# Selective scan: convolution folded into the projection, batch 1 prepared inside the loop, GpSimd takes part of the C products

## The reference

```
x  = norm(x)                      # L0a: RMS norm; L3a: layer norm with weight and bias
u, z = split(x @ W_in)            # 256 channels each
u  = silu(sum_j u[t-3+j] * conv_w[:, j] + conv_b)      # causal convolution, 4 taps
dt, B, C = split(u @ W_xproj)     # rank 8 (L0a) or 1 (L3a), 16 and 16
dt = softplus(dt @ W_dt + dt_bias)
for n in 16 states:               # a recurrence over the 512 positions
    s_n[t] = s_n[t-1] * exp(dt[t] * A_n) + dt[t] * u[t] * B_n[t]
    y[t]  += s_n[t] * C_n[t]
out = ((y + u * D) * silu(z)) @ W_out
```

## Time and profile before

| | us |
|---|---|
| median of 3 runs | 3445.13 (3442.0 to 3448.75) |
| profiled execution, its own time | 3442.52 |
| its span, first to last instruction | 3440.9 |
| busy PE, DVE, ACT, POOL | 2647.8, 1726.3, 1450.1, 576.3 |
| mean granted TensorE clock | 0.893 |

### The profile page before, as it was taken

The page is one execution under the profiler, slowest core; times in us unless marked ns, Lnnn a source line. Parts: engine busy times, 40 slices in busy tenths (PEclk is TensorE's granted clock), DMA queues, the critical chain, the costliest instruction groups (busy, mean ns, idle before and its releaser), DMA issues. The chain is left out here.

```text
span 3440.9 us, 33444 instructions
## 1 busy us (share of the span) xinstructions
PE 2647.8 (77%) x11658; PEld 1159.7 (34%) x11666; DVE 1726.3 (50%) x2715; ACT 1450.1 (42%) x2368; POOL 576.3 (17%) x564
## 2 busy tenths in 40 slices
PE   3567778999879789466745677889997897985677
PEld 1221264444334233123212212735443442431232
DVE  3867541555131721695648675425552227127955
ACT  2443502655234444443425445036552344444444
POOL 0432000000002411260006220000000024113500
PEclk8898968999979899799878989599999898997998
DMA  2002000000010210000000020000000102100000
GB/s 100 0 0 63 12 1 0 1 1 1 0 49 0 75 50 0 0 0 1 1 13 0 1 66 9 1 0 1 1 1 1 49 4 72 49 0 0 0 2 7
DMA packets 36752, 54.59 MB, mean 16 GB/s; under 512 B 7648, under 2 KB 19936, under 8 KB 36576
## 3 DMA queue, kind: packets, MB, share of 16 engines
q1 hardware_dynamic: 32224, 48.42, 4.3%
q10 hardware_dynamic: 4352, 3.94, 0.4%
HBM read 38.44 MB, written 13.63 MB: 15 GB/s over the span
## 5 line engine op out<-in xcount | busy, mean ns | idle before, releaser
L1709 ACT ACTIVATE L1b_pr<-ps,L1b_mneg 128x512 f32<-128x512 f32 x256 | 173.7, 683 | 195.7 <-DVE L1b_mneg L1748 195.7
L518 POOL TENSOR_TENSOR xs<-xs,L2f_part 128x512 f32<-128x512 f32 x32 | 40.5, 1265 | 1286.7 <-DVE L2f_part L507 1286.7
L90 ACT ACT_TABLE_LOAD x34 | 43.6, 1283 | 412.1 <-PEq L671 180.5
L1746 DVE TENSOR_REDUCE L1b_m<-ps 128x2 f32<-128x1024 f32 x128 | 156.8, 1225 | 105.0 <-PE ps L1613 101.0
L1046 POOL TENSOR_TENSOR L3a_db<-L3a_du,L3a_bs 128x1024 f32<-128x1024 f32 x64 | 150.4, 2354 | 225.2 <-ACT L3a_bs L1017 214.7
L1046 POOL TENSOR_TENSOR L0a_db<-L0a_du,L0a_bs 128x1024 f32<-128x1024 f32 x64 | 150.4, 2354 | 224.0 <-ACT L0a_bs L1017 213.5
L1416 ACT ACTIVATE L0b_pt<-ps 128x1024 f32<-128x1024 f32 x128 | 129.3, 1024 | 117.6 <-PE ps L1316 115.5
L1504 DVE TENSOR_REDUCE L0b_mx<-ps 128x1 f32<-128x512 f32 x256 | 159.0, 683 | 36.7 <-PE ps L1303 35.2
L1772 DVE COPY L1b_prt<-ps 128x512 f32<-128x512 f32 x128 | 88.5, 692 | 124.9 <-PE ps L1624 124.6
L1122 DVE TENSOR_TENSOR_SCAN L0a_hs<-ps,L0a_db 128x1024 f32<-128x1024 f32 x64 | 146.1, 2282 | 9.6 <-ACT ps L1009 8.0
L1122 DVE TENSOR_TENSOR_SCAN L3a_hs<-ps,L3a_db 128x1024 f32<-128x1024 f32 x64 | 146.1, 2283 | 9.4 <-ACT ps L1009 8.0
(11 more groups left out here) (556 smaller groups left out, 5471.1 us busy)
## 6 DMA issues: line engine op xcount, KB each, us to landing
L2f_w<-expert_dram SPq DMA_DIRECT2D x32, 256.0 KB, 3.0
L2g_w<-expert_dram SPq DMA_DIRECT2D x32, 256.0 KB, 3.0
weights<-w_dram SPq DMA_DIRECT2D x7, 852.5 KB, 9.3
L0b_qs<-stack_dram SPq DMA_DIRECT2D x32, 96.0 KB, 2.2
stack_dram<-L0b_cut SPq DMA_DIRECT2D x24, 128.0 KB, 2.2
L2b_qs<-stack_dram SPq DMA_DIRECT2D x32, 96.0 KB, 2.2
stack_dram<-L2b_cut SPq DMA_DIRECT2D x24, 128.0 KB, 2.1
L0b_ks<-stack_dram SPq DMA_DIRECT2D x28, 96.0 KB, 2.3
```

The lines of the kernel that those rows point to most:

```text
L1709: act.activation(pr[:, s % 2, h, :], g.ps[:, 2 * (s % 2) + h, :], ACT.Exp, bias=mneg[:, s % 2, h:h + 1], accum_out=total[:, u % 2, t, h:h ...
L1746: dve.tensor_reduce(m[:, s % 2, :], g.ps[:, 2 * (s % 2):2 * (s % 2) + 2, :], AX.X, ALU.max).then_inc(max_raw, 1)
```

## The change

- `prepare`: the blob of weights holds, for each block, the four taps repeated over 128 partitions (`_taps`, 1024 columns in place of `_cw` with 8). GpSimd multiplies them with the u half of the input projection, once, so that a tap and the projection are one weight matrix.
- The convolution: PE does it as four accumulating matmuls for each tile of 128 channels (`convolve`), over shifted windows of the normalized input `xin`, which has three zeros ahead. ACT's copy and DVE's eight tap instructions for each batch are gone. DVE reads the result from PSUM and halves it (`halve`).
- The second norm is made from the first one's variance v: its mean square is v/(v+eps), so that ACT makes 1/(v+eps) too, DVE multiplies it with v, and ACT takes the logarithm and exponential again. Squares, the mean on PE and variant 1's subtraction are gone.
- Batch 1: only its convolution, gate and u are ahead of the loop's first scan; x projection, dt, softplus, the bf16 split (on GpSimd, at step 6) and dt*u (on GpSimd, at step 10) are inside the loop over batch 0.
- C products: those of steps 5, 8, 11, ... 29 (9 of 32) are made by GpSimd (`weigh`), from a copy of C_n in SBUF that ACT makes (`take_c`). The loop's tiles in SBUF have three buffers; the decays still have two.
- The finish of batch 0 is made after step 17's scan.
- `load_exp_ln` stands ahead of the softplus logarithm; the second norm of variant 0's tail is started batch by batch.

```diff
@@ prepare
+            @block.gpsimd
+            def _(pool):
+                pool.wait_ge(loaded, 16 * cut)
+                for name in ("m0", "m3"):
+                    rows = g.w(name + "_taps").rearrange("p (j e) -> p j e", j=4)
+                    pool.tensor_tensor(rows, rows, bcast(g.w(name + "_in", 0, 2 * P), 1, 4), ALU.mult).then_inc(taps, 1)
@@ mamba
+    def on_pool(n):
+        return 5 <= n < steps - 1 and n % 3 == 2
...
@@ PE
+                def convolve(b, f):
+                    pe.wait_ge(x_in, b + 1)
...
+                    for j in range(4):
+                        mm = pe.matmul(g.ps[:, CONV[b] + f, :], g.w(w + "_taps", j * 2 * P + f * P, P), xin[:, b, j:j + T], start=(j == 0), stop=(j == 3))
+                    mm.then_inc(conv, 1)
...
+                def spread_c(n):
+                    if n >= 1:
+                        if on_pool(n - 1):
+                            pe.wait_ge(c_in, by_pool(n - 1))
+                        else:
+                            pe.wait_ge(weighed, by_dve(n - 1))
...
+                def add_state(n):
+                    b, s = n // NS, n % NS
+                    wait_weighed(pe, n)
+                    if n == 0:
+                        pe.wait_ge(dt_abs, 2 * NB)
+                    if s == 0 and b >= 1:
+                        pe.wait_ge(y_steps, b)
+                    for k in range(2):
+                        mm = pe.matmul(g.ps[:, SUM + k, :], g.w("ident"), hc[:, n % 3, k, :], start=(s == 0), stop=(s == NS - 1))
+                    mm.then_inc(summed, 1)
+                convolve(0, 0)
+                convolve(0, 1)
+                project_z(0)
+                project_x(0)
+                project_dt(0)
+                convolve(1, 0)
+                pe.wait_ge(conv_half, 3)
                 spread_b(0)
+                convolve(1, 1)
+                project_z(1)
+                pe.wait_ge(conv_half, 4)
+                spread_c(0)
                 spread_b(1)
+                project_x(1)
+                project_dt(1)
                 for n in range(steps):
                     if n + 2 < steps:
                         spread_b(n + 2)
                     if n + 1 < steps:
                         spread_c(n + 1)
+                    add_state(n)
@@ ACT
+                tanh_u(0, 0)
+                tanh_u(0, 1)
+                tanh_z(0)
+                take_x(0)
+                dt_magnitude(0)
+                dt_soft(0)
+                take_b(0)
                 act.wait_ge(cleared, 1)
                 decays(0)
+                tanh_u(1, 0)
+                tanh_u(1, 1)
+                tanh_z(1)
                 take_b(1)
+                take_x(1)
                 for n in range(steps):
                     if n + 1 < steps:
                         decays(n + 1)
+                    if on_pool(n):
+                        take_c(n)
+                    if n == 1:
+                        dt_magnitude(1)
                     if n + 2 < steps:
                         take_b(n + 2)
+                    if n == 3:
+                        dt_soft(1)
@@ POOL
+                def weigh(n):
+                    pool.wait_ge(scanned, n + 1)
+                    pool.wait_ge(c_in, by_pool(n))
+                    if n >= 3:
+                        pool.wait_ge(summed, n - 2)
+                    pool.tensor_tensor(hc[:, n % 3, :, :], hs[:, n % 3, :, :], bcast(cs[:, by_pool(n) % 2, :], 1, 2), ALU.mult).then_inc(weighed_pool, 1)
...
+                for n in range(steps):
+                    make_input(n)
+                    if n == 6:
+                        split_rows(1)
+                    if n == 10:
+                        pool.wait_ge(dt_sum, NB)
+                        pool.wait_ge(u_ready, 2 * NB)
+                        pool.tensor_tensor(du[:, 1, :, :], dt[:, 1, :, :], u[:, 1, :, :], ALU.mult).then_inc(dt_ready1, 1)
+                    if n >= 2 and on_pool(n - 2):
+                        weigh(n - 2)
@@ DVE
+                halve(0, 0)
+                make_u(0, 0)
+                halve(0, 1)
+                make_u(0, 1)
+                make_gate(0)
+                dt_positive(0)
+                split_rows(0)
+                halve(1, 0)
+                dt_add(0)
+                dve.wait_ge(gate_ready, 1)
+                dve.memset(g.ps[:, DECAY:DECAY + 4, 0:1], 0.0).then_inc(cleared, 1)
+                dve.wait_ge(dt_sum, 1)
+                dve.wait_ge(u_ready, 2)
+                dve.tensor_tensor(du[:, 0, :, :], dt[:, 0, :, :], u[:, 0, :, :], ALU.mult).then_inc(dt_ready, 1)
+                halve(1, 1)
+                make_u(1, 0)
+                make_u(1, 1)
+                make_gate(1)
                 for n in range(steps):
...
+                    if not on_pool(n):
+                        dve.wait_ge(scanned, n + 1)
+                        dve.wait_ge(c_row, n + 1)
+                        if n >= 3:
+                            dve.wait_ge(summed, n - 2)
+                        dve.tensor_tensor(hc[:, n % 3, :, :], hs[:, n % 3, :, :], bcast(g.ps[:, C_ROW, :], 1, 2), ALU.mult).then_inc(weighed, 1)
+                    if n == 0:
+                        dt_positive(1)
+                    if n == 5:
+                        dt_add(1)
+                    if n == NS + 1:
+                        finish(0)
+                finish(NB - 1)
```

More of the change, by code:

```diff
@@ L827, in mamba, with by_pool, by_dve @@
     KP = 96 + (8 if variant == 0 else 1)
+    eps, scale_of = (("eps6", "m0_rms1"), ("eps5", "m3_nw"))[variant]
+    steps = NB * NS
+    B_ROW, C_ROW, SUM, DECAY = 0, 1, 2, 4
+    CONV, GATE, XP, DT = (4, 0), (6, 2), (4, 2), ((5, 4), (3, 2))
+    def on_pool(n):
+        return 5 <= n < steps - 1 and n % 3 == 2
+    def by_pool(n):
+        return sum(on_pool(i) for i in range(n + 1))
+    def by_dve(n):
+        return n + 1 - by_pool(n)
     st = Stage(g, name)
@@ L844, in mamba @@
+        dbc = st.sb("dbc", [KP, NB, T])
+        rest = st.sb("rest", [64, T])
         bc = st.sb("bc", [96, NB, T], BF16)
         y = st.sb("y", [P, NB, 2, T])
[L846 to L855, removed]
@@ L863, in decay_banks, with wait_weighed @@
             return g.ps[:, at:at + 2, :]
[L865 to L878, removed]
+        def wait_weighed(engine, n):
+            if on_pool(n):
+                engine.wait_ge(weighed_pool, by_pool(n))
+            else:
+                engine.wait_ge(weighed, by_dve(n))
         with g.nc.Block() as block:
@@ L887, in _ @@
                 ln.tensor(pe)
[L888 to L905, removed]
+                def convolve(b, f):
+                    pe.wait_ge(x_in, b + 1)
+                    if b == 0 and f == 0:
+                        pe.wait_ge(pads, 1)
+                    if b == 1:
+                        pe.wait_ge(ln.centred, NB)
+                    for j in range(4):
+                        mm = pe.matmul(g.ps[:, CONV[b] + f, :], g.w(w + "_taps", j * 2 * P + f * P, P), xin[:, b, j:j + T], start=(j == 0), stop=(j == 3))
+                    mm.then_inc(conv, 1)
@@ new lines, in project_z, with project_x @@
+                def project_z(b):
+                    if b == 1:
+                        pe.wait_ge(again, NB)
+                    for f in range(2):
+                        mm = pe.matmul(g.ps[:, GATE[b] + f, :], g.w(w + "_in", (2 + f) * P, P), xin[:, b, 3:3 + T], start=True, stop=True)
+                    mm.then_inc(z, 1)
+                def project_x(b):
+                    pe.wait_ge(u_ready, 2 * b + 2)
+                    if b == 1:
+                        pe.wait_ge(gate_ready, 2)
@@ new lines, in _, with tanh_u @@
+                for b in range(NB):
+                    act.wait_ge(again, b + 1)
+                    act.activation(y[:, b, 1, :], y[:, b, 1, :], ACT.Ln, bias=g.w(eps)).then_inc(again_log, 1)
+                    act.wait_ge(again_log, b + 1)
+                    act.activation(y[:, b, 1, :], y[:, b, 1, :], ACT.Exp, scale=-0.5).then_inc(again_r, 1)
+                def tanh_u(b, f):
+                    act.wait_ge(conv_half, 2 * b + f + 1)
+                    act.activation(u[:, b, f, :], half[:, b, f, :], ACT.Tanh).then_inc(conv_tanh, 1)
@@ new lines, in _ @@
+                for n in range(steps):
[8 more added lines that the diff above has]
+                        weigh(n - 2)
+                for n in range(steps - 2, steps):
+                    if on_pool(n):
+                        weigh(n)
```

303 lines of the change are left out of this document (156 added, 147 removed).

## The result

The changed kernel took 3470.86 us, median of 4 runs (3465.36 to 3473.54), the kernel before beside it 3446.94 (3442.0 to 3452.36): ratio 1.0067, interval 1.0047 to 1.0087, so 0.5 to 0.9% slower. The forecast was 3468 us. The profiled execution took 3465.36 with a span of 3463.5, against 3442.52 and 3440.9: 22.6 more of span.

What follows compares the result with a forecast made beforehand. DVE was taken to set the loop's pace at 3.46 us a step. Four runs 10.6 us longer, less tails 2 x 8.5 and 2 x 1.3, plus 2.4 in `prepare`, give +25.2: 3468 us, range 3445 to 3495, chance 0.55.

Steps and rivals of the forecast that it cites:

- The ring: Loop: GpSimd stands still after its C product for addition, B row and copy; stall 4.5 us, period 13.9 against 10.4.
- the first rival: Loop: PE's clock stays up, stall 2.9 us, period 12.3, total 3361; chance 0.24 with mixtures of 3380 to 3435.
- Steps 8 to 29: Main part of the loop over batch 0, 21 steps: 105.7 us, before 77.5.
- The end: Loop steps 29 to 31, GpSimd's last C product, its addition, C row and last product: 11.9 us, before 10.4.
- Steps 0 to 8: Start of the loop, with batch 1's preparation inside it: 45 us, +16.4 (+7.9 at full clock throughout).
- The preparation: Ahead of the first scan in each run: scan 0 starts 35.4 us earlier, bounds 32.4 and 38.5.
- The second norm: In the preparation, made from the first norm's variance: gain 3.0 us, about 1.3 more in variant 1.
- The tail of variant 0: After the loop: four table loads go, fc1 starts 7.4 us earlier; 8.5 us saved taken in all.
- `prepare`: Once, loading weights: 1.04 MB more costs +2.4 us; GpSimd's two products 0, up to 4.7 if they block each other.
- third rival: DVE and GpSimd block each other in the `mamba` runs and `prepare`: up to +42 us, 3510; chance 0.10.
- The second: Loop: the serial chain doesn't bite and only work counts, 9.4 us a period, total 3296; chance 0.04.
- The fourth: Batch 1's work isn't covered by the loop, its waits stand ahead of loop work: +5 us a run, 3488; chance 0.07.

Runs made afterwards that it cites:

- e6: Changed kernel plus twenty redundant matmuls into the B row's bank ahead of each addition that waits for GpSimd: 3423.27 us, ratio 0.9916.
- e5: Changed kernel without GpSimd's two products of taps and projection in `prepare`: 3479.76 us from a single execution, not used; weights' landing to x load 9.86 us against 12.80.
- e1: Changed kernel with PE spreading the B row three steps ahead instead of two: 3383.44 us, ratio 0.9812.
- e7: Changed kernel with the B row three steps ahead and every addition one step later in PE's queue, behind both rows: 3298.77 us, ratio 0.9557.

## Why the prediction was right, point by point

**The ring.** As worked out: GpSimd stands still behind each of its C products for addition, row and copy. Stall 4.41 to 4.97, 4.69 on average, where 4.5 was taken (the bound above was 4.6 and was passed), period 13.7 to 14.7 where 13.9 was; at full clock 2.97 and 12.25 (`e6`) where the first rival had 2.9 and 12.3. The row behind the long pause was the right one to take. Steps 8 to 29: 107.3 against 105.7. The end: 11.86 against 11.9 (these two of the first run).

**Steps 0 to 8.** 43.1 against 45 in the first run: 1.9 too dear, while the rest of the loop was 1.6 too cheap, so the loop came out at 162.3 against 162.6. That is closer than the terms deserve. The other three take 45.0, 41.4 and 45.0.

**The preparation.** 35.8 gained, 35.4 forecast. The second norm gave 2.6 of the 3.0 taken: the convolution starts 11.4 us after the run's start (50.54 - 39.18) where the projection started 14.0 after it. The other 33 lie behind that point, in the terms from the convolution on; they weren't measured one by one.

**The tail of variant 0.** 9.8 against 8.5: fc1 7.2 earlier (7.4 forecast), and 2.6 further on, where 1.1 was allowed. Per run that is +0.1 on the first one by parts, the +0.2 above, where 10.6 - 8.5 = 2.1 was forecast. The third has -3.4: 36.0 saved ahead of the loop, a loop of 159.1 against 116.4, at a granted clock of 0.81 where the first run's had 0.77, and 10.0 saved in the tail. Variant 1: +9.5 and +8.5 against 10.6 - 1.3 = 9.3.

**`prepare`: the mis-sized term.** 5.2 against 2.4. The load itself was right, 22.26 - 19.90 = 2.4. The two products were put at 0, "up to 4.7 if they block each other", and they do: 2.9, shown by `e5`. The rule of the Trainium skill that the prediction set against itself ("SBUF — State Buffer", who interferes with whom) bears out in `e1`. The Trainium skill also states there that copy, cast and `tensor_scalar` can take the shared ports, where their operands meet its conditions, and that the engine that issued first keeps the other out for the whole instruction. The comparisons of `prepare` are such `tensor_scalar` instructions, and the trace agrees: they end at 24.73 and 27.03, just behind GpSimd's two products. The prediction had cited only the kind with two SBUF inputs; it had the 4.7 us of `prepare` in its third rival and nothing for them in its sum, and by that other sentence they wouldn't have stood at nothing. In the loop of after the rivalry cost little: once in each run DVE's sum of 1.22 us took 2.07, 2.63, 1.51 and 2.65, and a cast of 0.60 on GpSimd took 1.60 behind it in three of them.

**The sum.** 14.8 for the four runs where 4 x 10.6 - 2 x 8.5 - 2 x 1.3 = 22.8 was forecast, 5.2 for 2.4, and 2.5 in layers that nothing was said of: +22.6 against +25.2. The errors of -8.0, +2.8 and +2.5 partly cancel. The mechanism was right in the loop, the preparation and the tail, and left one thing out in `prepare`; that the total is off by 3 us only is luck.

**The rivals.** The first (clock stays up, 3361) is refuted for after by 0.79, and `e6`, which holds it up in the ring alone, gives 3423.27. The second (3296) needs another order of PE's queue; `e7` made it and got 3298.77. (Both rivals' sums take 19.6 us for the two tails, where 2 x (7.4 + 1.9) is 18.6; the 1 us changes nothing.) The third is real and small. The fourth: steps 0 to 8 cost 14.6 us more than before in the first run, which the sum had as 16.4, and nothing beyond that was seen.

## What to carry to other kernels

Before a piece of work moves to an idle engine, follow its result: who waits for it at the head of an in-order queue, and what stands behind the waiter that the idle engine itself will need. Cost the move by the ring and not by the engine's busy time, and put the wait behind everything that doesn't depend on it (here two small edits turned 0.7% lost into 4.4% gained). Then look at where the handed-over pieces end: every fourth product did better than every third, 5.0% gained, and most of what the profiles show of that in `mamba` is that the last piece no longer falls on the last steps, where DVE's finish waits behind it.

## What was unexpected of the hardware

- Filling half of PE's pause bought almost nothing: with 2.75 us of pause left in a period of 13.7 the granted clock was 0.88 and the addition took 3.4 to 3.6; with 0.52 left it was 1.00 and 1.98. 20 useless matmuls in a period made the kernel 48 us faster.
- DVE and GpSimd took turns by whole instructions where both read SBUF and DVE's was a comparison of a 128x128 tile or had two SBUF inputs: 0.28 became 2.38, 1.22 became 2.64, and GpSimd's 2.35 became 3.32. Beside a GpSimd memset, which reads nothing, a DVE product of two SBUF tiles kept its 0.69 (layer L0b of after, from 281.02). The scan and the C product, which read PSUM for one operand, kept 2.29 and 1.22 beside GpSimd all through the loop.
